# Reordered vector-side work in a batch-pipelined attention pass: inputs normalised earlier, GpSimd's queue and the order of ScalarE's exponentials changed, q's and k's second bias on ScalarE

## The reference, cut to what matters

```
# layer 0: attention over the 512 columns
Mn = Wn @ inorm(x) + bn ;  Mm = Wm @ inorm(ctx) + bm          # "m", two 128x512
A  = softmax(Mn^T @ Mm)                                        # 512 x 512, "S0"
x1 = Wo @ ((Wl @ ctx + bl) @ A^T) + bo + x                     # "u", then "out0"
# layer 1: 16 heads of 32, then an MLP
q  = (layer_norm(x1)*w + b) @ q_w + q_b ; k, v = ctx @ k_w + k_b, ctx @ v_w + v_b
P  = softmax(q k^T / sqrt(32), masked)                         # "S1", per head 128 x 128
hid = (P v) @ cproj_w + cproj_b + x1
out = hid + gelu(layer_norm(hid)*w + b @ fc_w + fc_b) @ proj_w + proj_b
```

## Time and profile before

| | us |
|---|---|
| median of 3 runs | 3171.57 |
| profiled execution, its own time | 3173.49 |
| its span, first to last instruction | 3171.7 |
| TensorE busy in the span | 2975.8 (94%) |
| VectorE, ScalarE, GpSimd busy | 1934.9, 1434.6, 784.2 |

### The profile page before, as it was taken

One profiled execution on the slowest core, in us unless ns is written; L12 is line 12 of the kernel. 1 busy time (PEld: TensorE's weight loads), 2 busy tenths in 40 slices (PEclk: granted clock), 3 DMA queues, 4 the chain that ended last, 5 costly groups with the idle time before them and its releaser, 6 DMA issues. The chain is left out here.

```text
span 3171.7 us, 55197 instructions
## 1 busy us (share of the span) xinstructions
PE 2975.8 (94%) x18551; PEld 2471.5 (78%) x18551; DVE 1934.9 (61%) x3769; ACT 1434.6 (45%) x4082; POOL 784.2 (25%) x742
## 2 busy tenths in 40 slices
PE   6899999999999999999996899999999999999999
PEld 4777777777777777777775688888888888888887
DVE  6788888888888888888885543333333333333332
ACT  5677766767676777777774211111111111111111
POOL 4443333334333333333332100000000000000000
PEclk9999999999999999999998899999999999999999
DMA  4344444444444444444445311111011111111110
GB/s 120 97 131 129 130 131 133 129 129 129 129 131 129 133 129 131 129 135 130 133 124 155 112 41 40 40 40 40 18 35 40 31 35 40 40 40 40 40 27 14
DMA packets 336372, 281.80 MB, mean 89 GB/s; under 512 B 149057, under 2 KB 247873, under 8 KB 336321
## 3 DMA queue, kind: packets, MB, share of 16 engines
q1 hardware_dynamic: 336320, 281.15, 31.7%
HBM read 164.68 MB, written 100.66 MB: 84 GB/s over the span
## 5 line engine op out<-in xcount | busy, mean ns | idle before, releaser
L1272 ACT ACTIVATE gl<-pre,fc_bias 128x512 f32<-128x512 f32 x256 | 176.6, 690 | 1118.5 <-PE pre L1357 1118.5
L1311 DVE CAST hT_hi<-gl 128x512 fp32r<-128x512 f32 x256 | 109.2, 427 | 838.2 <-ACT gl L1272 838.2
L634 ACT ACTIVATE rows<-bank,negmax 128x128 f32<-128x128 f32 x1024 | 360.5, 378 | 247.7 <-DVE negmax L778 247.7
L560 POOL TENSOR_TENSOR rows<-rows,rsum 128x512 f32<-128x512 f32 x256 | 263.6, 1040 | 364.4 <-DVE rsum L774 364.4
L1355 PE MATMUL pre<-yT_lo,rest_hi 128*128 128x512 f32 x768 | 298.8, 389 | 0.0
L1356 PE MATMUL pre<-yT_hi,rest_lo 128*128 128x512 f32 x768 | 298.8, 389 | 0.0
L1357 PE MATMUL pre<-yT_hi,rest_hi 128*128 128x512 f32 x768 | 298.8, 389 | 0.0
L1355 PE MATMUL acc<-rest_lo,hT_hi 128*128 128x512 f32 x768 | 298.8, 389 | 0.0
L1356 PE MATMUL acc<-rest_hi,hT_lo 128*128 128x512 f32 x768 | 298.8, 389 | 0.0
L1357 PE MATMUL acc<-rest_hi,hT_hi 128*128 128x512 f32 x768 | 298.8, 389 | 0.0
L177 POOL TENSOR_TENSOR rstd<-ve,neghalf 128x4 f32<-128x4 f32 x16 | 16.3, 1018 | 870.9 <-DVE ve L171 870.9
(11 more groups left out here) (162 smaller groups left out, 7874.2 us busy)
## 6 DMA issues: line engine op xcount, KB each, us to landing
p_turn<-rows SPq DMA_DIRECT2D x128, 512.0 KB, 3.0
p_blocks<-p_turn SPq DMA_DIRECT2D x256, 256.0 KB, 5.1
x_ctx<-in_x SPq DMA_DIRECT2D x64, 256.0 KB, 3.7
x_ctx<-in_ctx SPq DMA_DIRECT2D x64, 256.0 KB, 4.1
blocks<-in_ctx SPq DMA_DIRECT2D x256, 64.0 KB, 2.9
small<-in_x SPq DMA_DIRECT2D x64, 256.0 KB, 2.7
hidden<-hid SPq DMA_DIRECT2D x64, 256.0 KB, 2.0
rows<-hidden SPq DMA_DIRECT2D x16, 1024.0 KB, 5.5
```

What stands on the lines that cost most here:

```text
L560: pool.tensor_tensor(probs[:, :, r, :, :], probs[:, :, r, :, :], rsum1[:, r, :].unsqueeze(1).unsqueeze(3).to_broadcast([P, 4, 4, 32]), ALU ...
L634: act.activation(probs[:, :, r, c, :], by_chunk(S1_BANK[r])[:, c, :].rearrange("p (d b) -> p d b", b=32), ACT.Exp, bias=negmax1[:, r, c:c ...
L1272: act.activation(gl[:, i % 2, :], pre[i % 2][:], ACT.Gelu_apprx_tanh, bias=mlp.fc_bias[:, i:i + 1]).then_inc(gelu_done, 1)
```

## The change

- GpSimd: `x1_rstd` moves from ahead of normed_lo to behind it. x1b and ctxT_lo follow it, as they did.
- VectorE: the aggregates of the inputs' statistics stand right behind the statistics; normed stands ahead of outT_lo, the reciprocal of S0's sums and u_lo; xnT_lo stands ahead of `turn_probs(0)`; the second bias of k and q is gone; the lower half of q's weights (once, slot 2) moves from the slot's end to behind m_lo.
- ScalarE: xnT_hi stands between exp1(0) and exp1(1); normed_hi ahead of A's scaling; the second bias of k or q is two instructions ahead of ctxT_hi; the upper halves of q's and of cproj's weights (once each) move from the slot's end to ahead of exp1(2).
- TensorE: the same instructions; `qT_set[1]` and `kT_set[1]` now count two for a pair.

```diff
@@ GpSimd @@
-                if b1.exists():
-                    pool.wait_ge(x1_veps, b1.nth(1, 1))
...
-                    pool.tensor_tensor(x1_rstd[:], x1_ve[:], neghalf[:, 0:1], ALU.pow).then_inc(x1_rstd_ready, 1)
                 if ahead.exists():
                     for i in range(2):
                         pool.wait_ge(normed_hi_set, ahead.nth(2, i + 1))
...
                 if b1.exists():
+                    pool.wait_ge(x1_veps, b1.nth(1, 1))
...
+                    pool.tensor_tensor(x1_rstd[:], x1_ve[:], neghalf[:, 0:1], ALU.pow).then_inc(x1_rstd_ready, 1)
                     pool.wait_ge(x1_set, b1.nth(1, 1))
@@ ScalarE @@
+                def qk_bias(half):
+                    if s.parity == 0 and b1.exists() and b2.exists():
+                        act.wait_ge(k_done, b2.pair_nth(2, half + 1))
+                        for c in range(2):
+                            act.activation(kT[:, b2.quarter // 2, 2 * half + c, :],
+                                           bank[QK_BANK[half]][:, c * 2 * P:(c + 1) * 2 * P], ACT.Identity,
+                                           bias=vecs[:, 3, 2 * half + c:2 * half + c + 1]).then_inc(kT_set[half], 1)
...
                 exp1(0)
-                exp1(1)
                 if b2.exists():
                     act.wait_ge(xnT_turned, b2.nth(1, 1))
                     act.activation(pair_half(xnT_hi, b2), by_chunk(XN_BANK), ACT.Copy).then_inc(xnT_hi_set, 1)
+                exp1(1)
...
+                if b2.first():
+                    upper_halves(Q_W)
+                if b3.first():
+                    upper_halves(C_W)
                 exp1(2)
...
+                qk_bias(0)
                 exp1(3)
...
+                if ahead.exists():
+                    for i in range(2):
+                        act.wait_ge(normed_set, ahead.nth(2, i + 1))
+                        act.activation(normed_hi[:, i, :], normed[:, i, :], ACT.Copy).then_inc(normed_hi_set, 1)
                 if b0.exists():
                     act.wait_ge(rsum0_set, b0.nth(1, 1))
...
+                qk_bias(1)
@@ VectorE @@
                 sum1_reciprocal(1)
-                turn_probs(0)
                 if b2.exists():
                     dve.wait_ge(xnT_hi_set, b2.nth(1, 1))
                     lower(pair_half(xnT_lo, b2), by_chunk(XN_BANK), pair_half(xnT_hi, b2), xnT_lo_set)
+                turn_probs(0)
                 turn_probs(1)
...
+                if b2.first():
+                    lower_halves_of_q()
...
                     dve.bn_stats(in_stats[:, 1, :], ctx_in).then_inc(in_stat, 1)
+                    dve.wait_ge(in_stat, ahead.nth(2, 2))
...
+                        dve.bn_aggr(in_mv[:, i, :], in_stats[:, i, :]).then_inc(in_aggr, 1)
...
                 sum1_reciprocal(3)
@@ TensorE @@
-                    pe.wait_ge(qT_set[1], b4.pair_nth(1, 1))
+                    pe.wait_ge(qT_set[1], b4.pair_nth(2, 2))
```

More of the change, by code:

```diff
@@ L572, in slot @@
                     pool.tensor_tensor(in_rstd[:], in_ve[:], neghalf[:, 0:2], ALU.pow).then_inc(in_rstd_ready, 1)
-                if b1.exists():
-                    pool.wait_ge(x1_veps, b1.nth(1, 1))
-                    if b1.has_before(1):
-                        pool.wait_ge(x1n_set, (b1 + -1).nth(1, 1))
-                    pool.tensor_tensor(x1_rstd[:], x1_ve[:], neghalf[:, 0:1], ALU.pow).then_inc(x1_rstd_ready, 1)
                 if ahead.exists():
@@ L583, in slot @@
                 if b1.exists():
+                    pool.wait_ge(x1_veps, b1.nth(1, 1))
+                    if b1.has_before(1):
+                        pool.wait_ge(x1n_set, (b1 + -1).nth(1, 1))
+                    pool.tensor_tensor(x1_rstd[:], x1_ve[:], neghalf[:, 0:1], ALU.pow).then_inc(x1_rstd_ready, 1)
                     pool.wait_ge(x1_set, b1.nth(1, 1))
@@ L637, in exp1 @@
                                            accum_out=sum1[:, r, c:c + 1]).then_inc(exp1_done, 1)
+                def qk_bias(half):
[5 more added lines that the diff above has]
+                                           bias=vecs[:, 3, 2 * half + c:2 * half + c + 1]).then_inc(kT_set[half], 1)
+                    if s.parity == 1 and b3.exists() and b2.exists():
+                        act.wait_ge(q_done, b3.pair_nth(2, half + 1))
+                        for c in range(2):
+                            act.activation(qT[:, 2 * half + c, :],
+                                           bank[QK_BANK[half]][:, c * 2 * P:(c + 1) * 2 * P], ACT.Identity,
+                                           bias=q_bias[:, 2 * half + c:2 * half + c + 1]).then_inc(qT_set[half], 1)
                 exp1(0)
-                exp1(1)
                 if b2.exists():
@@ L703, in slot @@
                     act.activation(pair_half(ctxT_hi, b0), ctx_chunks, ACT.Copy).then_inc(ctxT_hi_set, 1)
[L704 to L707, removed]
             slots(act, slot, {1: lambda: upper_halves(V_W), LAST - 2: lambda: first_weights(0)})
@@ L830, in slot @@
                     dve.bn_stats(in_stats[:, 1, :], ctx_in).then_inc(in_stat, 1)
+                    dve.wait_ge(in_stat, ahead.nth(2, 2))
+                    dve.sem_inc(stats_seen, 1)
+                    for i in range(2):
+                        dve.bn_aggr(in_mv[:, i, :], in_stats[:, i, :]).then_inc(in_aggr, 1)
+                    dve.wait_ge(in_aggr, ahead.nth(2, 2))
+                    dve.tensor_scalar(in_ve[:], in_mv[:, :, 1], EPS, None, ALU.add).then_inc(in_veps, 1)
                 sum1_reciprocal(3)
@@ L840, in slot @@
                 if ahead.exists():
[L841 to L846, removed]
+                    dve.wait_ge(in_rstd_ready, ahead.nth(1, 1))
+                    if b0.exists():
+                        dve.wait_ge(m_done, b0.nth(2, 2))
+                        dve.wait_ge(normed_lo_set, b0.nth(2, 2))
+                    for i, src in enumerate((x_in, ctx_in)):
+                        dve.tensor_scalar(normed[:, i, :], src, in_mv[:, i, 0:1],
+                                          in_rstd[:, i:i + 1], ALU.subtract, ALU.mult).then_inc(normed_set, 1)
                 if b5.exists():
@@ L859, in slot @@
                     lower(u_lo[:], bank[U_BANK][:], u_hi[:], u_lo_set)
[L860 to L868, removed]
                 if b0.exists():
@@ L874, in slot @@
                                   blocks[:].rearrange("p (r c b) -> p c r b", c=DC, b=32)).then_inc(ctxT_turned, 1)
[L875 to L885, removed]
                 if b1.exists():
@@ L910, in slot @@
                     dve.tensor_tensor(hid[:], bank[C_BANK][:], x1b[:, b5.quarter, :], ALU.add).then_inc(hid_set, 1)
-                if b2.first():
-                    lower_halves_of_q()
             def statistics():
@@ L997, in slot @@
                 if s.parity == 0 and b4.exists() and b3.exists():
-                    pe.wait_ge(qT_set[1], b4.pair_nth(1, 1))
+                    pe.wait_ge(qT_set[1], b4.pair_nth(2, 2))
                 if s.parity == 1 and b3.exists() and b2.exists():
-                    pe.wait_ge(kT_set[1], b3.pair_nth(1, 1))
+                    pe.wait_ge(kT_set[1], b3.pair_nth(2, 2))
                 if b4.exists():
```

## The result

The changed kernel took 3131.02 us at the median of four runs (3129.93 to 3131.31), the kernel before 3172.23 (3171.36 to 3174.21) beside it: ratio 0.9869, interval 0.9852 to 0.9886. It is faster by 41.2 us; the forecast was a gain of 37, to 3135, in a range of 3108 to 3160. The profiled execution took 3130.87, its span 3129.1, against 3171.7.

The account below looks back on a forecast made before the run. No engine is full; TensorE, busy 92.4%, stops some 2 us a slot for late operands. Pairs 31.9 + start 6 - end 1 = 37 us off, so 3135 us, with an 8-in-10 range of 3108 to 3160.

Parts of the forecast that it names:

- The first wait goes: TensorE's wait for x1n: with normed_lo out of the way, its turn comes 1.41 us earlier in K slots, 1.48 in Q slots.
- rival 3: GpSimd: normed_lo ends after x1's variance, the first wait stays, new waits are pure loss; 3180 to 3224 us, chance 0.07.
- The new wait: VectorE: the second reciprocal waits for exp1(1), now behind xnT_hi; all from there comes 1.07 us later against the turn.
- K slot: Slot with k: -1.41 for x1n, +1.07 through m_lo, +0.25 for the aggregates through at_lo, sum -0.09 us.
- Q slot: Slot with q: -1.48 for x1n, +0.47 as half 0 of q waits longer for xnT_lo, sum -1.01 us.
- Bias: Second bias moved from VectorE to ScalarE, 0.84 us a slot there: no loss or gain in time.
- 29 pairs: Full slots 5 to 62: 29 x (0.09 + 1.01) = 31.9 us gained.
- Start: Slots 2 to 5: 9.4 us of x1n waits, 3.5 coming back where q's weights now stand; net 6 us gained.
- End: Slot 65, a Q slot without a first wait, loses about 1 us.
- x1n beside GpSimd: VectorE's x1n keeps its long form beside GpSimd: turn at 4.15 us instead of 4.10, 3 us over 60 slots.
- 1: VectorE late in both slots, S0's maxima delayed in Q slots: pairs gain 0.35 to 0.8 less; 3144 to 3158, chance 0.14.
- 2: exp1(1) holds nothing back: a pair gains 3.99 us, 116 us in all; 3050 with the start, halfway 3090; chance 0.05.

Follow-up runs that it names:

- e2: Kernel before with only GpSimd's x1_rstd moved behind the two normed_lo; normed and normed_hi stay late: 3085.72 us, ratio 0.9726.
- e4: Kernel before with only ScalarE's xnT_hi put between exp1(0) and exp1(1): 3245.06 us, ratio 1.0231.
- e1: Changed kernel with exp1(1) ahead of xnT_hi again on ScalarE: 3055.55 us, ratio 0.9634.
- e3: Changed kernel with VectorE's second reciprocal moved from ahead of xnT_lo to behind m_lo: 3054.27 us, ratio 0.9633.
- e6: Changed kernel with the inputs' aggregates and in_ve moved from ahead of S0's maxima to behind the third maximum: 3127.70 us, ratio 0.9861.
- e5: Changed kernel with the second bias of k and q back on VectorE: 3129.91 us, ratio 0.9865.
- e7: Changed kernel with the once-only halves of q's and cproj's weights back at the ends of slots 2 and 3: 3135.93 us, ratio 0.9886.
- e9: Changed kernel with VectorE's second reciprocal behind m_lo and the aggregates behind S0's third maximum: 3048.29 us, ratio 0.9609.

## Why the prediction was right

- *The first wait goes, 1.41 us in a K slot and 1.48 in a Q slot.* This came as forecast, and e2 shows that GpSimd's order does it by itself. The prediction took the moves of normed and normed_hi into the reason and let rival 3 say that a normed_lo later than the variance of x1 brings the whole wait back. That was too strict. In e2 normed and normed_hi stand where they were, GpSimd's two normed_lo end at 1014.39 us, x1_rstd follows at 1014.83 and x1b at 1015.48, 0.77 after S1's start (1014.71); in the kernel before it was 2.63 after. x1b must wait for hid in any case, which there ends at 1015.40. What the early normed does, by the traces, is keep normed_lo away from the mask instruction.
- *The new wait, 1.07 us on VectorE.* Measured are 2.67 - 1.64 = 1.03 us. e4 shows it alone; e1 and e3 each take it away, from one end and from the other. In both K slots of the timeline the turn of A starts 10.17 us after S1 (961.04 to 971.21), where the prediction's numbers give 5.51 - 1.41 + 1.07 + 5.03 = 10.20. TensorE's wait for m_lo is 1.20 us where about 1.0 was forecast.
- *K slot, -0.09.* Measured is -0.17, 25.51 against 25.68. The prediction took 0.25 for the aggregates, paid in full because at_lo already held TensorE. The cost came as 0.18 here (0.37 against 0.19), and e6 takes it back. But at_lo held TensorE only in every other K slot before. In the others the wait is new, 0.27, and the slot went from 25.60 to 25.41 us.
- *Q slot, -1.01.* Measured is -1.05, 25.65 against 26.70; the wait for xnT_lo was to be 1.57 and is 1.56.
- *Bias, 0.* Right (e5); in the loop S1 never waits for kT or qT.
- *29 pairs, 31.9 us.* From the start of S1 in slot 5 to its start in slot 63 the kernel before took 1516.89 us (123.91 to 1640.80) and the changed one 1483.05 (116.35 to 1599.40): 33.8 us.
- *Start, 6.* Slot 5 begins 7.6 us earlier. x1n's wait in slot 3 fell from 5.56 to 1.14, and what I priced at 3.5 cost less: TensorE's waits for at_lo in slot 2 and for k's bias ahead of slot 3 grew by 0.44 us each (0.71 to 1.15, 0.89 to 1.33). e7 has the weights back and keeps the second of them, 1.33, so that one is not the weights'.
- *End, -1.* Slot 65 did lose 1.07 us (17.94 to 19.01). Slot 63, which I had not counted, gained 1.04, so the attention pass lost 0.3 behind the 29 pairs. The rest of the span's 42.6 us, 1.5, lies behind the last hid, where no instruction changed. In the profiled executions of this document that stretch is between 1409.2 and 1411.0 us long, in no order that follows the edits, so these 1.5 us are no merit of the change. Together that is 33.8 + 7.6 - 0.3 + 1.5 = 42.6 us of the span, where 37 were forecast; the medians differ by 41.2.
- *x1n beside GpSimd.* The prediction cited the GPSIMD Engine Reference of the Trainium skill (Specifications), by which GpSimd shares its memory interfaces with VectorE. The 3 us that this could have cost did not come: x1n starts 2.57 us after S1 in the Q slot, lasts 1.32 beside ctxT_lo, and the turn still starts at 4.09. Over the changed kernel it takes 534 to 1429 ns, with a median of 1183. Where such a slowdown does cost time is e2, in the mask instruction.
- *Rivals.* 1: at_lo held TensorE only in K slots. 2: its 116 us need exp1(1) out of the way; e1, e3 and e9 are that case, with 3055.55, 3054.27 and 3048.29, where it said 3050. 3: normed_lo got out with 2.08 us to spare (1.7 forecast), and by what e2 shows, a normed_lo just behind the variance would not have brought the whole first wait back.

## What to carry to other kernels

When an engine runs in order, an edit that brings one instruction forward must be followed through everything left behind the wait it now imposes, on the other engines too: here xnT_hi went ahead of exp1(1), and a 0.16 us reciprocal that waits for exp1(1) carried the delay into the two results that TensorE waits for. Such a small instruction, if it waits for another engine, is worth trying behind those that the busiest engine needs: here this gained 77 us. A change of several edits that gains should be taken apart: here one edit of several, alone, gained twice what all together did.

## What the runs showed of the hardware

A VectorE instruction of 0.21 us (the mask's, 128x128, bf16 from uint8, one tensor operand and a constant) took 1.22 us at the median in e2, up to 1.33, when a GpSimd instruction of 128x512 float32 with two operands (normed_lo) ran beside it, and ended 0.08 to 0.09 us after it. So it went for 60 of the 64; the four without GpSimd beside them took 0.21 to 0.22. In the changed kernel, with nothing beside it, its median is 0.208. GpSimd's own instructions stayed at 2.54 us for two. VectorE's x1, with one operand in PSUM and one in SBUF, started 0.01 us after GpSimd's and kept its 0.75; the statistics behind it kept their 0.69.

x1n shows the same (128x512 float32, two scalars for each partition). The one that had no GpSimd instruction beside it took 0.54 us in the kernel before and 0.53 in the changed one. In the loops of both kernels each ran beside ctxT_lo, for 1.40 to 1.41 us before and 1.12 to 1.43 after, and ended 0.27 to 0.29 us after ctxT_lo, whenever it had started: started 0.14 to 0.17 us after it, it took 1.40 or more, started 0.45 after it, 1.12.
